# A two-layer adapter kernel: a new order for the start-up loads and for the first work of ScalarE, VectorE and TensorE

## What is computed

```
def _L0_cond_ref(x, thresholds, deltas, zero_points):
    gi = jnp.sum(jnp.abs(x)[..., None] <= thresholds, axis=-1)
    ...
    x_quant = jnp.clip(jnp.round(x / d) + zp, 0, N_LEVELS - 1)
    x_dequant = (x_quant - zp) * d
    return jnp.where(gi == G, jnp.float32(0), x_dequant)
...
x = x + _L0_ffn_ref(_L0_cond_ref(x, ...), router_w, A, B)      # top 2 of 4 experts, rank 16
x = x + _L1_ffn_ref(_L1_cond_ref(x, itok, W, lora_A, lora_B_w), gate, kernel, bias, ...)
```

## Time and profile before

| | us |
|---|---|
| median of 3 runs | 455.98 |
| the 3 runs | 455.03, 456.48, 455.98 |
| the profiled execution | 455.03 |
| its span (first to last instruction) | 453.2 |

### The profile page before, as it was taken

How to read it: one execution, slowest core, us unless ns; L and a number is a source line. 1 busy time by engine, 2 the same in 40 slices (tenths; PEclk the granted TensorE clock), 3 DMA queues, 4 the chain that set the end, 5 groups by cost and what they waited for, 6 DMA issues and landing times.

```text
span 453.2 us, 5629 instructions
## 1 busy us (share of the span) xinstructions
PE 445.7 (98%) x2166; PEld 348.3 (77%) x2166; DVE 392.8 (87%) x392; ACT 357.7 (79%) x296; POOL 7.9 (2%) x11
## 2 busy tenths in 40 slices
PE   8979999999999999999999999999999999999997
PEld 8847778888878887778767877777778777867883
DVE  1696979999999999999999999999987999899410
ACT  1579999946989969898997899959697899778002
POOL 0000000000000000100000000000200000000000
PEclk9999999999999999999999999999999999999999
DMA  7999535200562153214125107105414003101102
GB/s 271 358 311 410 140 82 175 58 1 0 167 204 92 53 135 100 78 39 156 59 93 162 59 25 232 58 2 162 152 31 132 29 29 140 58 1 46 48 1 93
DMA packets 36124, 50.35 MB, mean 111 GB/s; under 512 B 26658, under 2 KB 26914, under 8 KB 33826
## 3 DMA queue, kind: packets, MB, share of 16 engines
q1 hardware_dynamic: 35090, 42.66, 29.6%
q0 software_dynamic: 1008, 7.34, 4.8%
HBM read 39.51 MB, written 10.49 MB: 110 GB/s over the span
## 4 chain that ended last, share of the span: by engine, by line
PE 92%; SPq 4%; DMA 3%; issue 1%; ACT 0%
PE bank L1090 13%; PE bank L1092 13%; PE bank L1091 13%; PE bank L970 6%; PE bank L1067 6%; PE bank L1027 6%; PE bank L1032 6%; PE bank L1028 6%; PE bank L998 6%; PE bank L939 5%; DMA lb<-lb_in 3%; PE bank L1088 2%; PE bank L994 2%; PE bank L1005 1%; PE bank L958 1%; SPq L327 1%
## 5 line engine op out<-in xcount | busy, mean ns | idle before, releaser
L680 DVE COPY_PREDICATED val<-inside,val 128x2048 f32<-128x2048 uint8 x56 | 143.3, 2559 | 0.3
L439 ACT ACTIVATE val<-level,shift,small 128x2048 f32<-128x2048 int16 x64 | 133.9, 2093 | 3.7 <-PE bank L970 3.7
L426 ACT ACTIVATE level<-xq,inv 128x2048 int16<-128x2048 f32 x64 | 127.7, 1997 | 0.6
L1090 PE MATMUL bank<-p_hi,x_hi 128*128 128x512 f32 x256 | 102.8, 402 | 0.0
L1092 PE MATMUL bank<-p_hi,x_lo 128*128 128x512 f32 x256 | 100.1, 391 | 0.0
L1091 PE MATMUL bank<-p_lo,x_hi 128*128 128x512 f32 x256 | 100.0, 391 | 0.0
L662 DVE TENSOR_SCALAR val<-val,width,unshift 128x2048 f32<-128x2048 f32 x64 | 87.2, 1363 | 3.1 <-ACT val L439 3.0
L671 DVE TENSOR_SCALAR inside<-absx,thr 128x2048 uint8<-128x2048 f32 x56 | 72.7, 1299 | 0.0
L1090 PEld LDWEIGHTS bank<-p_hi,x_hi 128*128 128x128 f32 x256 | 48.1, 188 | 17.1 <-issue 8.5
L1091 PEld LDWEIGHTS bank<-p_lo,x_hi 128*128 128x128 f32 x256 | 48.1, 188 | 10.5 <-issue 0.7
L1092 PEld LDWEIGHTS bank<-p_hi,x_lo 128*128 128x128 f32 x256 | 48.1, 188 | 10.5
(11 more groups left out here) (98 smaller groups left out, 447.0 us busy)
## 6 DMA issues: line engine op xcount, KB each, us to landing
xs<-xt_in SPq DMA_DIRECT2D x8, 1024.0 KB, 4.9
wst<-w_in SPq DMA_DIRECT2D x14, 512.0 KB, 5.0
xq<-xt_in POOLq DMA_DIRECT2D x7, 1024.0 KB, 6.6
out_t<-ost SPq DMA_DIRECT2D x14, 512.0 KB, 4.0
la<-la_in SPq DMA_DIRECT2D x4, 512.0 KB, 5.4
kst<-k_in SPq DMA_DIRECT2D x4, 512.0 KB, 13.7
lb<-lb_in SPq DMA_DIRECT2D x4, 512.0 KB, 14.4
kst<-k_in SPq DMA_DIRECT2D x1, 2048.0 KB, 10.8
```

The costliest lines, as they stand in the source:

```text
L426: nc.scalar.activation(level[:, g % 2], xq[:, c % 2], ACT.Copy, scale=inv[:, group(g)]).then_inc(levels_made, 1)
L439: nc.scalar.activation(val[:, turn(c, g)], level[:, g % 2], ACT.Relu, bias=shift[:, group(g)], scale=par[:, 1, group(g)]).then_inc(raised, 1)
L680: nc.vector.copy_predicated(val[:, acc(c)], inside[:, g % 2], val[:, turn(c, g)]).then_inc(merged, 1)
L1090: mm(o, x_hi[:, s, k, at], p_hi[:, h, k], start=False, stop=False)
```

## The change

The change has five parts.

- **SP's queue.** `ab_raw` goes ahead of `bw`; the first W tile goes between the second and the third quarter of `kst`; the second W tile and the first input `xq[:, 0]` go behind the label reads and the eight `alt` loads.
- **PE's start.** All eight first-half `k_update` are done ahead of `u_product(0)` instead of inside and behind it. In step 7 the last second-half `k_update` is issued behind o = 4 instead of o = 6.
- **weight_hi(0) and weight_lo(0)** move from ahead of the `kst` work into it: on ACT ahead of the fifth `kp_hi`, on DVE behind the eight `k_add` and the first `kp_lo`.
- **ACT's first quantizing.** `u_out(0)`, `p_out(0)`, the first `rows_out`, `u_out(1)` and `weight_hi(2)` used to stand between or ahead of the first quantizing operations; now they are part of the loop over steps and stand behind them. In every step of the loop `u_out(n)` stands behind the first of the step's pairs instead of ahead of them.
- **The tables** TAKEN and LAGS get other numbers: which steps take a pair, and when the gates of the first sequences are due.

```diff
-    LAGS = [(2, 4, 5, 6, 7, 9), (2, 3, 3, 4, 4, 5), (3, 4, 4, 5, 6, 8), (3, 6, 6, 7, 8, 10), (2, 5, 5, 6, 8, 9), (2, 3, 3, 3, 4, 5), (1, 2, 2, 4, 4, 5), (2, 2, 3, 3, 4, 6)]
-    TAKEN = [0, 1, 0, 2, 2, 2, 1, 1, 1, 1, 1, 1, 1, 1, 1, 1, 1, 2]
+    LAGS = [(2, 4, 5, 6, 7, 9), (3, 3, 4, 5, 5, 6), (3, 4, 4, 5, 6, 7), (3, 5, 5, 6, 7, 9), (2, 5, 5, 6, 7, 8), (2, 3, 3, 3, 4, 5), (1, 2, 2, 4, 4, 5), (2, 2, 3, 3, 4, 6)]
+    TAKEN = [0, 0, 2, 2, 2, 2, 1, 1, 0, 1, 1, 1, 1, 1, 1, 1, 1, 2]
...
+            sp.dma_start(ab_raw, a["ab"]).then_inc(ab_in, 16)
             sp.dma_start(bw, a["bw"]).then_inc(bw_in, 16)
-            sp.dma_start(ab_raw, a["ab"]).then_inc(ab_in, 16)
-            sp.dma_start(wst[0], w_v[0]).then_inc(w_in[0], 16)
             for i in range(KPARTS):
+                if i == KPARTS // 2:
+                    sp.dma_start(wst[0], w_v[0]).then_inc(w_in[0], 16)
                 sp.dma_start(kst[:, i * KO:(i + 1) * KO], k_v[0, :, i * KO:(i + 1) * KO]).then_inc(k_part_in[i], 16)
...
-            sp.dma_start(xq[:, 0], x_v[0]).then_inc(x_first_in, 16)
-            sp.dma_start(wst[1], w_v[1]).then_inc(w_in[1], 16)
             sp.wait_ge(itok_in, 16)
...
+            sp.dma_start(wst[1], w_v[1]).then_inc(w_in[1], 16)
+            sp.dma_start(xq[:, 0], x_v[0]).then_inc(x_first_in, 16)
             for g in range(NG):
...
                 for o in range(KT):
+                    if h == 0 and o == 4:
+                        weight_hi(0)
                     act.wait_ge(k_sum, h * KT + o + 1)
...
-            weight_hi(0)
             kp_split(0)
...
+            levels(0, 0)
+            raise_levels(0, 0)
+            act.wait_ge(bwp_made, 1)
+            weight_hi(1)
+            magnitude(0)
+            levels(0, 1)
+            raise_levels(0, 1)
+            levels(0, 2)
...
-            levels(0, 0)
-            raise_levels(0, 0)
-            act.wait_ge(bwp_made, 1)
-            weight_hi(1)
-            u_out(0)
-            p_out(0)
-            for i in range(HALVES):
-                rows_out(i)
-            magnitude(0)
-            levels(0, 1)
-            u_out(1)
-            raise_levels(0, 1)
-            weight_hi(2)
-            levels(0, 2)
             for n in range(STEPS):
...
-                if n == KT:
+                if n == 1 or n == KT:
                     u_out(n - 1)
-                if n > 1:
+                if n:
                     p_out(n - 1)
-                if 1 < n <= NG:
+                if 0 < n <= NG:
...
-                if 1 < n < KT - 1:
+                for c, g in GROUPS[n + 1][:1]:
+                    quant(c, g)
+                if 0 < n < KT - 1:
                     u_out(n)
-                for c, g in GROUPS[n + 1]:
+                if n == 1:
+                    weight_hi(load_of(n + 1))
+                for c, g in GROUPS[n + 1][1:]:
                     quant(c, g)
...
                 for o in range(KT):
+                    if h == 0 and o == 1:
+                        weight_lo(0)
                     dve.wait_ge(kp_hi_made, h * KT + o + 1)
...
-            weight_lo(0)
             for o in range(KT):
                 k_add(0, o)
...
+            pe.wait_ge(ab_lo_made, 2)
+            for o in range(KT):
+                k_update(0, o)
+
             def u_product(n):
...
-                    if n == 0 and o == 2:
-                        pe.wait_ge(ab_lo_made, 2)
-                        for k in range(len(kfirst)):
-                            k_update(0, k)
...
-                    else:
-                        for k in range(len(kfirst), KT):
-                            k_update(0, k)
...
-                    if n == KT - 1 and o == KT - 2:
+                    if n == KT - 1 and o == KT // 2:
                         k_update(1, n)
```

## The result

| | before | after |
|---|---|---|
| median of the runs, us | 456.1 (455.03 to 456.48, 4 runs) | 464.09 (463.82 to 464.54, 4 runs) |
| ratio | | 1.0174, 95% interval 1.016 to 1.0188 |
| profiled execution, us | 455.03 | 463.36 |
| its span, us | 453.2 | 461.6 |

The changed kernel is 8.0 us slower. The forecast was 463.4, with a range from 459.8 to 467.0.

A forecast was written before the change was run, and what follows sets the result against it. PE was taken to bound the kernel, with no later wait to absorb new ones. Terms 0 + 5.5 + 0.9 + 1.0 = 7.4 us on a median of 455.98 gave 463.4 us, range 459.8 to 467.0.

The forecast's parts named there:

- What bounds the kernel: PE, busy 98% of the span; its waits total 4.4 us, all before 33 us, so any new wait adds in full.
- When `xq` lands: Start-up loads: `xq`, now directly ahead of the first `lb`, lands at about 31.5 instead of 25.0, 6.5 us later.
- that rival: Start-up loads: the slow stretch does not move with `alt`, `xq` lands at 29.3, total 461.2 us; chance 0.12.
- ACT's chain: ACT from `xq` to `u_out(1)`: 18.5 us of work, so `u_out(1)` starts at 50.0 and ends at 50.4.
- Up to the first `lb` product, 0: PE's start-up to 32.8 us: `lb` hides losses and gain, worth 0; bounds 0 to +0.5, or -0.7.
- Step 1, +0.3: PE at step 1: `w_lo` on DVE ends at 38.1 against PE's 37.80, costing 0.3 us.
- `u_product(2)`, +5.5: PE at `u_product(2)` waits for `u_out(1)` and stands 5.5 us later, the 0.3 of step 1 included.
- The later waits, +0.9 and +1.0: Steps behind `u_product(2)`: 0.9 us once for `u_out(2)`, then 1.0 (bounds 0 and 2) for later `u_out` rounds.
- the clock rival: PE's clock falls in the wait at `u_product(2)`: net +0.9 to +2.8 us, 464.3 to 466.2; chance 0.17.
- signs of being wrong: `xq` before 29, PE's `u_product(2)` wait under 3 us, clock below full in 50 to 56 us, or waits in the sequences' part.
- signs of being right: ACT waits some 6 us for `xq`; PE's longest wait at `u_product`; about 1 us for `bw`, under 1 at a later `u_product`.
- The rival with `xq` early: Start-up loads: `xq` lands by 25.5, only 1.4 us are left, 457.0 at most; not slower, chance 0.06.

The follow-up runs named there:

- 128-partition run: Changed kernel with the eight `alt` loads of 32 partitions replaced by eight of the same size into all 128, from `lb`: 460.2 us.
- `bw`-first run: Changed kernel with `bw` issued ahead of `ab` again: 464.28 us.
- run with `xq` back: Changed kernel with `xq` issued ahead of the label reads again, W tile 1 left behind `alt`: 459.03 us.
- two tries with W tile 1 late: Kernel before with W tile 1 behind the first `lb`, `magnitude(0)` ahead of `weight_hi(1)`; the second adds four idle-time matmuls ahead of step 0: 456.24 and 456.21 us.
- new-order, old-queue kernel: Changed kernel with SP's start-up queue in the order of the kernel before: 458.01 us.

## Why the prediction was right

**What bounds the kernel**: right. PE had no wait to absorb a new one, and the shift of 8.5 us at 64 us is the shift of the end, 8.4.

**When `xq` lands**: 31.5 forecast, 32.0 measured. The reasoning by bytes ahead of it in the queue held, and the slow bytes moved with `alt`; the 128-partition run took that rival away.

**ACT's chain**: 18.5 us forecast from rows of before, 18.56 measured (32.11 to 50.67). The end of `u_out(1)` was forecast at 50.4 and was 51.05, nearly all of it from the later `xq`.

**Up to the first `lb` product, 0**: nearly. The `bw` wait was 1.5 us, not 1.0, and I did not count that the clock falls there, which made L928's work 1.6 us longer. `lb`'s cover of 0.7 us was used up, and PE came 0.55 us late. It did not reach the end: PE then stood idle for 5.1 us at `u_product(2)`.

**Step 1, +0.3**: it came. Step 1 started at 38.82 instead of 37.80, 1.0 late: 0.55 brought along from `lb`, and the rest at `w_lo`, with a wait of 0.23 in the trace. This too was covered by the wait at `u_product(2)`.

**`u_product(2)`, +5.5**: 6.3 measured, by 0.6 of later `u_out(1)` and a start of the passes 0.15 us behind its end.

**The later waits, +0.9 and +1.0**: ACT lost what was forecast, but PE did not show it as waits. `u_out(2)` came 11.65 us behind `u_out(1)`, where 11.8 was forecast. By ACT's end of `u_out(5)` alone, 97.75 and the 0.15 that PE needs behind it, `u_product(6)` would start at 97.9, 8.15 behind the 89.75 of the kernel before:

```profile
89.75 3.62 PE L939 MATMUL bank<-aefft,wst 128*128 128x256 f32 x16
```

Less the 6.3 of `u_product(2)` that is 1.9, the forecast's own sum. What stands in the trace in its place is the clock rival: the granted clock fell in the 5 us wait, PE lost 2.2 us in the passes of `u_product(2)`, and found ACT ready ever after. So one of the prediction's own signs of being wrong came true, a granted clock below full between 50 and 56 us, and one of its signs of being right did not, a wait at a later `u_product`. I gave the clock's fall 0.17 and priced it at +0.9 to +2.8 net. The chance was too small and the price too high: 0.3 in the traces, at most 0.9 by the medians. That the fall moved the total so little is in part luck, since the 2.2 us lost happened to be about what ACT made PE wait for anyway. My reason against the fall, that a wait of 2.06 us had left the clock alone, was weak: in the second profile of the same kernel a wait of 1.9 us did not. And my price for a low clock was read from the passes at L883, 0.41 us each, over which the trace grants the full clock (1.00 from 0 to 7 us); why these are slow stays open. The size was still right: at a granted 0.52, from 50 to 57 us of the `bw`-first run, 16 passes took 6.57 us, 0.41 each.

**The rival with `xq` early**: for `xq` at 25.5 the prediction has 1.4 us left (and writes 457.0, where its sum gives 457.4). The run with `xq` back is nearly this case, with `xq` in use from 25.91, and measured 2.4 above before.

**Sum**: 7.4 forecast, 8.0 measured by the medians, 8.4 by the two spans. Of the 8.5 by which `u_product(6)` is late, the 6.3 of `u_product(2)` stood at 5.5 in the forecast (0.65 for the later `u_out(1)`, 0.15 for the start behind it), the 1.9 behind it at 1.9, and the clock's 0.3 at nothing.

## What to carry to other kernels

Judge a load that is moved back by who stands behind its consumer in an engine's fixed order, not by the consumer's own due time: here quantizing was not urgent, but `u_out` and `weight_hi` stood behind it on ACT. Two edits that each eat into the same lead don't add: the queue cost 2.9 us, the order 2.0, both 8.0, so test them apart before blaming one. A load's landing in a full queue is the sum of the bytes ahead of it, each at its own rate; those of `alt` and `ab_raw` counted nearly double here (232 and 228 GB/s against 372 to 425). And before pricing a loss on one engine, ask whether it would have stood waiting for another in that time: here 2.2 us of slow passes cost 0.3.

## What the runs showed of the hardware

- Loads into 32 partitions moved at 232 GB/s with the DMA engines fully busy; with loads of the same bytes over 128 partitions in their place the queue moved 372 to 419 GB/s, and `xq` landed 3.3 us earlier. A load into 96 partitions also moved at 228 GB/s. What of a transfer sets its rate stays open.
- The granted clock of PE fell in waits of very different length: in the changed kernel around a wait of 1.5 us, in the kernel before once with a wait of 1.9 us and once not with 2.06, and with `xq` back not with one of 1.5 us at `u_product(2)` (1.00 from 40 to 60 us). With work in the three waits (`bw`, step 0, `u_product(2)`) it did not fall up to 60 us. What decides between the short ones stays open.
- The start-up loads vary between executions of the same queue order: `xq`, issued at 8.2 to 8.7 us in the order of the kernel before, took 16.8 and 16.5 us to land in its two profiles, 19.4 and 18.5 us in the two tries with W tile 1 late, and 20.0 us in the one with the new order on the engines. That such executions make up the upper end of before's spread (454.54 to 459.1 us beside the first experiments) is likely and was not shown. The transfer's row of the new-order, old-queue kernel:

```profile
xq<-xt_in SPq DMA_DIRECT2D x1, 1024.0 KB, 20.0
```
